# Cross attention with a second branch on one core: two staging places and the order of the last batch changed

## The chip, the cores and the metric

The kernel runs on one core of one Trainium2 chip. The metric is the device time of one execution in microseconds (us). A core has a matrix engine (PE, with weight loads shown apart as PEld), VectorE (DVE), ScalarE (ACT), GpSimd (POOL), and SyncE (SP), which here only issues transfers. SP and ACT issue DMAs; 16 DMA engines move the data.

## The reference, cut to what matters

There are 16 batches of 100 tokens x (640 wide) and a context of 722 rows (384 wide), of which the last 4 are apart. All data are float32.

```
query = x @ Wq;  key = enc @ Wk;  val = enc @ Wv          # enc: 718 context rows
hs    = attention(query, key, val)                        # 8 heads of 80
ca_q1 = (ca^T @ Wq_ca)[100 picked rows]                   # ca: the last 4 context rows
ca_hs1= attention(ca_q1, x, x)
ca_hs2= attention(ca_hs1 @ Wq, ca @ Wk_ca, ca @ Wv_ca)
out   = (hs + ca_hs2) @ Wout + b_out + x
```

## The kernel before, in words

Each float32 matrix product is done on split operands: a high part in a rounded format and a low part, the difference to the original. Nearly every tile is therefore first copied to its high part by ACT, and the low part is a subtraction on DVE or POOL. In the code `..._high` is the copy on ACT and `..._low` the subtraction. Three products (high x high, high x low, low x high) make one.

**Stage 1** (0 to some 80 us) computes the queries of all batches, transposed, in four groups of 400 columns (`query(g, j)`, j = 0 to 4 the five blocks of 128 rows, j = 5 a narrow block g, from which the second branch makes its scores). The results are split into tiles that are later used for something else: `q_out(g, j, p)` names the place. They are then stored to DRAM (`store_q2`, `store_g2`, `store_q3` on ACT's queue) and read again batch by batch. Groups 2 and 3 are not done when batch 0 starts; group 3 is woven into batch 0. The place of g of group 2 is slot 5 of `PT_keep`, columns 0 to 399, where the transposed probabilities of heads 0 to 3 come to lie in batch 0. So `pt_high(0, 0)` waits for all eight stores of group 2.

**A batch** on PE is an order written out by hand, `batch(i, first, last)`, one such function for each engine. Batch 0 is `first`, 1 to 14 are a loop, 15 is `last`. The parts are:

- `keys(i, f)`: block f of the keys, from encT (transposed context), into psS. `k_high`, `k_low` split it into kT, and SP's `lift` copies rows of kT to kstack, head by head, by DMA.
- `scores(i, h)`: head h's scores into psS, from kstack. DVE takes the row maximum (`rowmax`), ACT the exponential (`expo`), DVE divides by the sum (`norm`).
- `turn(i, h)`: PE transposes the probabilities into psT; `pt_high`, `pt_low` move them to PT.
- `context(i, u)`: a piece (u = 0 to 5) of probabilities times encN into psB; `u_high`, `u_low` move it to UT. Every piece uses the same bank of psB and waits for the `u_low` before it.
- `values(i, half)`: UT times Wv, plus the second branch, into psT; `hs_copy` on ACT and `hs_add` on DVE add its two halves and free psT. `turn` of heads 0 and 4 waits for that.
- `b2_...`: the second branch. `b2_pt_high(i, half)`, `b2_pt_low(i, half)` split its transposed probabilities of four heads.

Context pieces 2 to 5 and the values of batch i - 1 are done within batch i. Behind PE there is always the same rule: engines work strictly in the order of their function, so an instruction that waits holds all behind it on that engine.

In batches 0 to 14, `keys(i + 1, 0)` lies between `values(i - 1, 1)` and `turn(i, 4)`, and `context(i, 0)` behind `scores(i, 7)`. Batch 15 has no next keys; there `context(15, 0)` takes the place of those keys, and the output product `tile(0, 0)` starts in the place of the last keys. Wout is loaded (`load_wo`) into the room of encT, in two parts, 960 and 640 KB, and split by `wo_high` and `wo_low`. The context rows encN come in three pieces (`load_enc(i, c)`, 384 KB each); `enc_high(i, c)` on ACT is their split, and waits for `rawN{c}`.

The lines that the rows below show: 755 scores, 780 keys, 796 turn, 815 to 827 context, 848 to 855 values, 981 query blocks, 868 second-branch scores, 1190 expo, 1201 pt_high, 1219 split of encT, 1226 enc_high, 1257 b2_pt_high, 1612 rowmax, 1636 hs_add, 1675 b2_pt_low, 1772 low part of a query block, 377 load_enc, 391 and 394 lift, 500 load_wo.

Of the kernel before, what the change touches and what calls it, by code (L numbers as in the profile page):

```python
# [27 lines left out]
FT = H // 128  # L28
KT = 6
# [66 lines left out]
def program(nc, x, xT, encT, encN, caT, asel, Wq, WqT, Wk, Wv, WqcaBD, Wkca, Wvca, Wout, bout, out,  # L96
            q_d, g_d, v2_d, m_d, hs_d):

    with ExitStack() as ctx:
# [115 lines left out]
        SLOT3 = (0, 1, 2, 3, 5, 4)  # L215

        def q_out(g, j, p):

            rows = slice(0, 128 if j < FT else (2 - p) * HT)
            return PT_keep[p][rows, j, 0:GT] if g < 3 else PT_keep[p][rows, SLOT3[j], HALFCOLS]  # L220
# [43 lines left out]
        stage1_stores = "qst0 qst1 qst2 qst3a qst3b v2st mst0 mst1 mst2"  # L264
# [69 lines left out]
        with nc.Block() as block:  # L334
            @block.sync
            def _(sp):
# [172 lines left out]
                def batch(i, first=False, last=False):  # L509
                    if last:  # L510
                        load_enc(i, 0)
                    else:
                        load_encT(i + 1, 0, first)
# [7 lines left out]
                    if last:  # L521
                        sp.wait_ge(s["encT"], PARTS * (B - 1))
                        load_wo(0)
                    lift(i, 3)
                    if last:
                        load_enc(i, 2)
                    else:
# [5 lines left out]
                    if last:  # L533
                        sp.wait_ge(s["wolo"], 2)
# [9 lines left out]
                    tail_pt0(i)  # L544
                    tail_enc(i)
# [19 lines left out]
                for n, k in (("qst1", 6), ("qst2", 8), ("qst3a", 8), ("qst3b", 4)):  # L565
                    sp.wait_ge(s[n], 16 * k)
# [171 lines left out]
            def _(pe):  # L738
# [321 lines left out]
                def batch(i, first=False, last=False):  # L1060
# [40 lines left out]
                    if last:  # L1101
                        context(i, 0)
                    else:
                        keys(i + 1, 0)
# [3 lines left out]
                    if not last:  # L1108
                        context(i, 0, first)
# [73 lines left out]
            def _(act):  # L1183
# [10 lines left out]
                def pt_high(i, h, first=False):  # L1194
                    act.wait_ge(s["pt"], HEADS * i + h + 1)
                    if first and h == 0:
                        act.wait_ge(s["qst2"], 16 * 8)
                    if first and h == 4:
                        act.wait_ge(s["qst3a"], 16 * 8)
                        act.wait_ge(s["qst3b"], 16 * 4)  # L1200
# [137 lines left out]
                def wv_high(c):  # L1338
                    if c == 0:
                        act.wait_ge(s["wvin"], 16)  # L1340
                        act.wait_ge(s["q"], NP * GROUPS)
                    nc.scalar.activation(Wv_s[0][:, c, :], wv_raw[:, c, :], ACT.Copy).then_inc(s["wvhi"], 1)
# [7 lines left out]
                def store_g2():  # L1350
                    act.wait_ge(s["qlo"], NP * 2 + NP)
                    for p in range(2):
                        rows = slice(2 * p * HT, (2 + p) * HT)
                        act.dma_start(raw(g_d[rows, 2 * GT:3 * GT]), raw(q_out(2, FT, p))).then_inc(s["qst2"], 16)

                def store_q3(j):
                    to = s["qst3a" if j < 4 else "qst3b"]
# [6 lines left out]
                def batch(i, first=False, last=False):  # L1364
# [37 lines left out]
                    expo(i, 4)  # L1402
                    b2_pt_high(i, 1)
# [38 lines left out]
                    if last:  # L1442
                        wo_high(3)
# [590 lines left out]
```

## Time and profile before

| | |
|---|---|
| median of 3 runs | 975.27 us (973.79 to 976.19) |
| the profiled execution | 974.73 us |
| its span, first to last instruction | 973.0 us |
| mean granted clock of TensorE | 0.996 |
| PE busy | 960.6 us (99%), 6634 matmuls |
| DVE, ACT, POOL busy | 701.8 (72%), 491.6 (51%), 343.0 us (35%) |
| DMA queue of SP | 181.53 MB, 75.9% of 16 engines' span |
| DMA queue of ACT | 13.35 MB, 4.4% |

A table of this kind gives averages over stages with different limits. Times of single instructions are counted from the start of the span. Batch 0 runs from some 80 to 138 us, then each batch takes 50.9 us, and batch 15 lies between some 853 and 904 us. What follows is the rest of the output product.

### The profile page before, as it was taken

How to read it: one execution, taken by the hardware profiler on the slowest of the kernel's cores; microseconds unless marked ns; L12 is line 12 of the kernel's file. 1: busy time of each engine (PE TensorE's matmuls, PEld its weight loads, DVE VectorE, ACT ScalarE, POOL GpSimd, SP SyncE). 2: the span in 40 equal slices, each digit the busy share in tenths (PEclk: the TensorE clock that was granted, in tenths of full speed). 3: DMA queues.
4: the chain of work that ended last, by engine and by line, in shares of the span. 5: the costliest groups of instructions: out<-in, count | busy, mean ns of one | idle time of the engine just before them, and what ended most of it. 6: DMA issues, size and time to landing. Idle time of an engine off the chain costs nothing.

```text
span 973.0 us, 21012 instructions
## 1 busy us (share of the span) xinstructions
PE 960.6 (99%) x6634; PEld 943.3 (97%) x6634; DVE 701.8 (72%) x1260; ACT 491.6 (51%) x911; POOL 343.0 (35%) x302
## 2 busy tenths in 40 slices
PE   9999899999999999999999999999999999999998
PEld 8999899999999999999999999999999999998998
DVE  5545677777777777787777787777777777876445
ACT  6534556454555555564646363736464545555111
POOL 5223363334343425160615152433333343415000
PEclk9999999999999999999999999999999999999999
DMA  8989987797779777768796879788887978797455
GB/s 266 301 276 264 285 193 213 163 225 176 201 182 206 185 198 185 198 186 193 194 193 194 190 195 185 209 174 218 175 221 163 217 174 206 178 207 183 116 170 167
DMA packets 157625, 195.21 MB, mean 201 GB/s; under 512 B 81056, under 2 KB 111712, under 8 KB 157600
## 3 DMA queue, kind: packets, MB, share of 16 engines
q1 hardware_dynamic: 150000, 181.53, 75.9%
q10 hardware_dynamic: 7600, 13.35, 4.4%
q8 instruction: 15, 0.25, 0.1%
q14 instruction: 10, 0.08, 0.0%
HBM read 82.74 MB, written 19.95 MB: 106 GB/s over the span
## 4 chain that ended last, share of the span: by engine, by line
PE 91%; DMA 3%; SPq 2%; DVE 1%; ACT 1%; POOL 1%; issue 0%; ACTq 0%; POOLq 0%
PE psS L780 24%; PE psB L815 18%; PE psB L820 9%; PE psS L755 8%; PE psT L796 6%; PE psS L930 5%; PE psT L848 4%; PE psT L854 3%; PE psB L825 2%; PE psB L827 2%; PE psB L981 2%; DMA kstack<-kT 1%; PE psS L1055 1%; PE psB L903 1%; PE psB L880 1%; PE psT L855 1%
## 5 line engine op out<-in xcount | busy, mean ns | idle before, releaser
L780 PE MATMUL psS<-encT_keep,Wk_keep 128*128 128x360 f32 x1440 | 254.1, 329 | 0.0
L780 PEld LDWEIGHTS psS<-encT_keep,Wk_keep 128*128 128x128 f32 x1440 | 237.5, 188 | 0.7
L1190 ACT ACTIVATE probs<-psS,negmax 100x718 f32<-100x718 f32 x128 | 110.1, 860 | 131.8 <-DVE negmax L1612 131.7
L815 PE MATMUL psB<-PT_h,encN_h 128*128 128x400 f32 x480 | 169.5, 353 | 0.0
L815 PE MATMUL psB<-PT_l,encN_h 128*128 128x400 f32 x480 | 165.6, 345 | 0.0
L635 POOL TENSOR_TENSOR encT_keep<-encT_raw,encT_keep 128x718 fp32r<-128x718 f32 x45 | 83.6, 1857 | 180.7 <-ACT encT_keep L1219 176.2
L1629 DVE TENSOR_TENSOR PT_l<-psT,PT_h 128x600 fp32r<-128x600 f32 x128 | 99.6, 778 | 40.5 <-ACT PT_h L1201 36.8
L626 POOL TENSOR_TENSOR Mbd<-Mbd,fmask 128x320 fp32r<-128x320 f32 x48 | 41.8, 871 | 213.3 <-DMA Mbd<-m_split 210.7
L1612 DVE TENSOR_REDUCE negmax<-psS 100x1 f32<-100x720 f32 x128 | 114.8, 897 | 1.3 <-PE psS L755 1.3
L1201 ACT ACTIVATE PT_h<-psT 128x600 fp32r<-128x600 f32 x128 | 85.7, 669 | 42.7 <-PE psT L796 38.9
L1623 DVE TENSOR_SCALAR probs<-probs,inv 100x718 f32<-100x718 f32 x128 | 102.1, 798 | 4.5
L820 PE MATMUL psB<-PT_h,encN_l 128*128 128x400 f32 x480 | 103.6, 345 | 0.8 <-POOL encN_l L650 0.8
L1214 ACT ACTIVATE kT<-psS 128x718 fp32r<-128x718 f32 x80 | 61.6, 770 | 80.6 <-PE psS L780 78.0
L1645 DVE TENSOR_TENSOR UT<-psB,UT 128x400 fp32r<-128x400 f32 x96 | 55.1, 574 | 65.4 <-ACT UT L1243 65.3
L1243 ACT ACTIVATE UT<-psB 128x400 fp32r<-128x400 f32 x96 | 48.2, 502 | 93.8 <-PE psB L827 93.8
L1640 DVE TENSOR_TENSOR kT<-psS,kT 128x718 fp32r<-128x718 f32 x80 | 72.1, 901 | 27.1 <-ACT kT L1214 25.5
L815 PEld LDWEIGHTS psB<-PT_h,encN_h 128*128 128x128 f32 x480 | 90.3, 188 | 0.6 <-ACT encN_h L1226 0.3
L755 PE MATMUL psS<-kstack,qstack_h 120*100 120x360 f32 x256 | 87.8, 343 | 2.9 <-DMA kstack<-kT 2.9
L815 PEld LDWEIGHTS psB<-PT_l,encN_h 128*128 128x128 f32 x480 | 90.4, 188 | 0.0
L820 PEld LDWEIGHTS psB<-PT_h,encN_l 128*128 128x128 f32 x480 | 88.2, 188 | 1.2 <-POOL encN_l L650 1.2
L796 PE MATMUL psT<-ident,probs 100*128 100x100 f32 x768 | 86.9, 249 | 0.4 <-DVE P L1689 0.4
L796 PEld LDWEIGHTS psT<-ident,probs 100*128 100x128 f32 x768 | 79.3, 140 | 5.1 <-DVE P L1689 0.8
(259 smaller groups left out, 1787.4 us busy)
## 6 DMA issues: line engine op xcount, KB each, us to landing
kstack<-kT SPq DMA_DIRECT2D x64, 448.8 KB
kstack<-kT SPq DMA_DIRECT2D x192, 112.2 KB
enc_raw<-in_encN_dram SPq DMA_DIRECT2D x48, 384.0 KB, 4.6
encT_raw<-in_encT_dram SPq DMA_DIRECT2D x45, 359.0 KB, 3.9
kstack<-kT SPq DMA_DIRECT2D x32, 359.0 KB
kstack<-kT SPq DMA_DIRECT2D x32, 269.2 KB
kstack<-kT SPq DMA_DIRECT2D x32, 179.5 KB, 3.5
kstack<-kT SPq DMA_DIRECT2D x64, 89.8 KB, 3.8
```

The source lines that it names most:

```text
L635: nc.gpsimd.tensor_tensor(eT[1][:, c, :], rawT[:, c, :], eT[0][:, c, :], ALU.subtract).then_inc(s["encT"], 1)
L755: mm = pe.matmul(psS[score_slot[h]][0:S, half, 0:HALF], qst[p][:, h, :], kst[:, p, h % SLOTS, k0:k0 + HALF], start=(p == 0), stop=(p == 1))
L780: mm = pe.matmul(keys_in(f, first)[:, half, 0:HALF], w[:, c, f * 128:(f + 1) * 128], e[:, c, k0:k0 + HALF], start=(j == 0), stop=(j == 3 * ...
L796: mm = pe.transpose(psT[0:KP, k // 3, (k % 3) * S:(k % 3 + 1) * S], P[h % PRING][0:S, k * KP:(k + 1) * KP], ident[0:S, 0:S])
L815: pe.matmul(psB[:, 1, 0:RH], eN[0][:, k, cc], PT[p][:, k, rows], start=(k == 0 and p == 0), stop=False)
L820: pe.matmul(psB[:, 1, 0:RH], eN[1][:, k, cc], PT[0][:, k, rows], start=False, stop=False)
L1190: nc.scalar.activation(halves(P[h % PRING][0:S, 0:KEYS]), without_overlap(psS[score_slot[h]], S), ACT.Exp, bias=negmax[:, h:h + 1], accum_ ...
L1201: nc.scalar.activation(PT[0][:, :, h * S:(h + 1) * S].rearrange("p (a k) n -> p a k n", a=2), psT[0:KP, :, 0:3 * S].rearrange("p a (k n) - ...
L1612: nc.vector.tensor_reduce(negmax[:, h:h + 1], tile_in(h), AX.XY, ALU.max, negate=True).then_inc(s["negmax"], 1)
L1623: nc.vector.tensor_scalar(P[h % PRING][0:S, 0:KEYS], P[h % PRING][0:S, 0:KEYS], inv[:, h:h + 1], None, ALU.mult).then_inc(s["norm"], 1)
L1629: nc.vector.tensor_tensor(o[1], psT[0:KP, :, 0:3 * S].rearrange("p a (k n) -> p a k n", k=3), o[0], ALU.subtract).then_inc(s["ptlo"], 1)
L1640: nc.vector.tensor_tensor(halves(kT[f % 2][1][:, :]), without_overlap(keys_in(f, first), 128), halves(kT[f % 2][0][:, :]), ALU.subtract).t ...
```

## The change

Four things are changed.

1. g of group 2 is staged in slot 5, columns 400 to 799 of `PT_keep`, and g of group 3 in the room of the first rows of Wv (`Wv_s[p][:, 0]`), which hold the first block of Wq until the queries are done. Block 4 of group 3 goes to slot 4. The semaphores are named anew: `qst2` (q of group 2, 6 stores), `gst2` (g of group 2), `qst3` (q of group 3, 10 stores), `gst3`. `pt_high(0, 0)` waits for `qst2` alone, `pt_high(0, 4)` for `qst3` and `gst2`, `wv_high(0)` for `gst3`.
2. In batch 0, `b2_pt_high(0, 1)` stands ahead of `expo(0, 4)` on ACT and `b2_pt_low(0, 1)` ahead of `rowmax(0, 4)` on DVE.
3. In batch 15 SP issues Wout's first part at the batch's beginning, the third piece of encN behind `lift(15, 4)`, and `tail_enc` ahead of `tail_pt0`.
4. In batch 15 `context(15, 0)` stands behind `scores(15, 7)` on PE, and ACT and DVE follow: ACT does head 4's copy and exponential 7, then Wout's blocks 3 and 4, then `u_high(15, 0)`.

```diff
-        SLOT3 = (0, 1, 2, 3, 5, 4)
+        SLOT3 = (0, 1, 2, 3, 4)
         def q_out(g, j, p):
             rows = slice(0, 128 if j < FT else (2 - p) * HT)
+            if j == FT and g == 2:
+                return PT_keep[p][rows, KT - 1, HALFCOLS]
+            if j == FT and g == 3:
+                return Wv_s[p][rows, 0, 0:GT]
             return PT_keep[p][rows, j, 0:GT] if g < 3 else PT_keep[p][rows, SLOT3[j], HALFCOLS]
@@ SP, batch
                     if last:
+                        sp.wait_ge(s["encT"], PARTS * (B - 1))
+                        load_wo(0)
                         load_enc(i, 0)
...
-                    if last:
-                        sp.wait_ge(s["encT"], PARTS * (B - 1))
-                        load_wo(0)
                     lift(i, 3)
-                    if last:
-                        load_enc(i, 2)
-                    else:
+                    if not last:
                         load_encT(i + 1, 2, first)
...
                     lift(i, 4)
                     if last:
+                        load_enc(i, 2)
                         sp.wait_ge(s["wolo"], 2)
                         load_wo(1)
...
-                    tail_pt0(i)
-                    tail_enc(i)
+                    if last:
+                        tail_enc(i)
+                        tail_pt0(i)
+                    else:
+                        tail_pt0(i)
+                        tail_enc(i)
@@ PE, batch
-                    if last:
-                        context(i, 0)
-                    else:
+                    if not last:
                         keys(i + 1, 0)
                     turn(i, 4, first)
                     b2_scores2(i)
                     scores(i, 7)
-                    if not last:
-                        context(i, 0, first)
+                    context(i, 0, first)
@@ ACT
                     if first and h == 0:
-                        act.wait_ge(s["qst2"], 16 * 8)
+                        act.wait_ge(s["qst2"], 16 * 6)
                     if first and h == 4:
-                        act.wait_ge(s["qst3a"], 16 * 8)
-                        act.wait_ge(s["qst3b"], 16 * 4)
+                        act.wait_ge(s["qst3"], 16 * 10)
+                        act.wait_ge(s["gst2"], 16 * 2)
...
                         act.wait_ge(s["q"], NP * GROUPS)
+                        act.wait_ge(s["gst3"], 16 * 2)
                     nc.scalar.activation(Wv_s[0][:, c, :], wv_raw[:, c, :], ACT.Copy).then_inc(s["wvhi"], 1)
...
-                    expo(i, 4)
-                    b2_pt_high(i, 1)
+                    if first:
+                        b2_pt_high(i, 1)
+                        expo(i, 4)
+                    else:
+                        expo(i, 4)
+                        b2_pt_high(i, 1)
...
+                    if not last:
+                        enc_high(i, 2)
+                        k_high(i + 1, 0)
+                    if first:
+                        expo(i, 7)
+                    pt_high(i, 4, first)
+                    if not first:
+                        expo(i, 7)
                     if last:
                         wo_high(3)
                         wo_high(4)
-                        u_high(i, 0)
-                    else:
-                        enc_high(i, 2)
-                        k_high(i + 1, 0)
-                    if first:
-                        expo(i, 7)
-                    pt_high(i, 4, first)
-                    if not first:
-                        expo(i, 7)
-                    if not last:
-                        u_high(i, 0)
+                    u_high(i, 0)
                     pt_high(i, 5)
@@ DVE, batch
-                    rowmax(i, 4)
-                    b2_pt_low(i, 1)
+                    if first:
+                        b2_pt_low(i, 1)
+                        rowmax(i, 4)
+                    else:
+                        rowmax(i, 4)
+                        b2_pt_low(i, 1)
...
-                    if last:
-                        u_low(i, 0)
-                    else:
+                    if not last:
                         k_low(i + 1, 0)
...
-                    if not (first or last):
+                    if not first:
                         u_low(i, 0)
```

## Rows read from the trace of the kernel before

**Rows 1.** Waits of PE: engine, line, waited for, us in total, times, longest.

```profile
PE psB L981 <- DVE PT_l L1772: 2.9, 2, 2.0
...
PE psS L755 <- DMA kstack<-kT: 2.9, 2, 1.7
```

**Rows 2.** Stretches: length, busy PE PEld DVE ACT POOL, granted clock, DMA share, GB/s.

```profile
99.00:112.00 13.00, 10.07 (x65) 9.47 (x64) 8.73 (x19) 8.15 (x15) 5.21 (x3) 1.00 0.97 255
...
188.00:850.00 662.00, 662.00 (x4668) 652.47 (x4667) 511.49 (x937) 354.92 (x663) 251.73 (x208) 1.00 0.81 193
...
850.00:879.00 29.00, 29.00 (x202) 28.66 (x200) 21.87 (x40) 15.48 (x29) 5.98 (x5) 1.00 1.02 203
```

**Rows 3.** Timeline of batch 0, ACT, PE and DVE: start, length, engine, [idle before it].

```profile
85.62 1.33 ACTq L1347 DMA_DIRECT2D q_split<-PT_l  x1
...
94.41 0.50 ACT L1257 ACTIVATE P1T<-psB 100x400 fp32r<-100x400 f32 x1
...
96.92 0.67 ACT L1201 ACTIVATE PT_h<-psT 128x600 fp32r<-128x600 f32 x1 [2.02 <-DMA g_split<-PT_l]
...
101.26 0.45 PE L981 MATMUL psB<-encN_h,Wv_h 128*128 128x400 f32 x1 [1.96 <-DVE PT_l L1772]
...
106.35 0.80 ACT L1219 ACTIVATE encT_keep<-encT_raw 128x718 fp32r<-128x718 f32 x1
...
107.19 0.90 DVE L1612 TENSOR_REDUCE negmax<-psS 100x1 f32<-100x720 f32 x1
...
110.70 0.42 PE L981 MATMUL psB<-encN_h,Wv_h 128*128 128x400 f32 x1 [0.97 <-DVE PT_l L1772]
```

**Rows 4.** Chain that ended last: start, length, what; for a DMA from issue to landing.

```profile
88.78 8.06 DMA g_split<-PT_l
...
872.49 8.54 DMA kstack<-kT
```

**Rows 5.** DMA issues from 84.5 to 87 us: count, KB, us to landing.

```profile
q_split<-PT_l ACTq DMA_DIRECT2D x1, 200.0 KB, 6.1
```

**Rows 6.** Timeline of batch 15, PE.

```profile
881.17 0.38 PE L755 MATMUL psS<-kstack,qstack_h 120*100 120x360 f32 x1 [1.69 <-DMA kstack<-kT]
...
885.69 0.36 PE L815 MATMUL psB<-PT_h,encN_h 128*128 128x400 f32 x1
...
888.82 0.68 PE L796 MATMUL psT<-ident,probs 100*128 100x100 f32 x6
...
892.36 0.45 PE L815 MATMUL psB<-PT_h,encN_h 128*128 128x400 f32 x1
```

**Rows 7.** Timeline of batch 15, DMA issues on SP's queue.

```profile
862.57 0.46 SPq L500 DMA_DIRECT2D encT_raw<-in_Wout_dram  x1
...
869.41 0.52 SPq L377 DMA_DIRECT2D enc_raw<-in_encN_dram  x1
...
874.09 1.53 SPq L394 DMA_DIRECT2D kstack<-kT  x2
...
877.97 0.37 SPq L500 DMA_DIRECT2D encT_raw<-in_Wout_dram  x1
```

**Rows 8.** DMA issues in 869:870, 877:879 (batch 15) and 825:828 (batch 14), us to landing last.

```profile
enc_raw<-in_encN_dram SPq DMA_DIRECT2D x1, 384.0 KB, 9.7
...
encT_raw<-in_Wout_dram SPq DMA_DIRECT2D x1, 640.0 KB, 9.2
...
enc_raw<-in_encN_dram SPq DMA_DIRECT2D x2, 384.0 KB, 4.3
```

**Rows 9.** Timeline of batch 15, ACT and DVE.

```profile
879.59 1.57 ACT L1226 ACTIVATE encN_h<-enc_raw 128x768 fp32r<-128x768 f32 x2
...
883.02 0.86 ACT L1190 ACTIVATE probs<-psS,negmax 100x718 f32<-100x718 f32 x1 [0.41 <-DVE negmax L1612]
...
886.42 0.57 DVE L1636 TENSOR_TENSOR hs<-psT,hs 80x400 f32<-80x400 f32 x1 [2.87 <-ACT hs L1248]
```

**Rows 10.** Stretch of batch 15 behind the hole, columns as in rows 2.

```profile
882.00:886.00 4.00, 4.00 (x31) 4.00 (x30) 1.47 (x2) 1.67 (x6) 3.84 (x3) 0.57 0.68 183
```

More of the change, by code:

```diff
@@ L262, in program @@
             enc0hi enc0lo wvhi wvlo hhi hlo qhi qlo k2 k2hi k2lo v2 v2hi v2lo m mhi mlo"""
-        stage1_stores = "qst0 qst1 qst2 qst3a qst3b v2st mst0 mst1 mst2"
+        stage1_stores = "qst0 qst1 qst2 gst2 qst3 gst3 v2st mst0 mst1 mst2"
         names = " ".join((loads, products_done, exps_and_highs, steps_and_lows, splits, tails, stage1_loads, stage1,
@@ L564, in _ @@
                 batch(0, first=True)
-                for n, k in (("qst1", 6), ("qst2", 8), ("qst3a", 8), ("qst3b", 4)):
+                for n, k in (("qst1", 6), ("qst2", 6), ("gst2", 2), ("qst3", 10), ("gst3", 2)):
                     sp.wait_ge(s[n], 16 * k)
@@ L1353, in store_g2 @@
                         rows = slice(2 * p * HT, (2 + p) * HT)
-                        act.dma_start(raw(g_d[rows, 2 * GT:3 * GT]), raw(q_out(2, FT, p))).then_inc(s["qst2"], 16)
+                        act.dma_start(raw(g_d[rows, 2 * GT:3 * GT]), raw(q_out(2, FT, p))).then_inc(s["gst2"], 16)
                 def store_q3(j):
-                    to = s["qst3a" if j < 4 else "qst3b"]
+                    to = s["qst3" if j < FT else "gst3"]
                     act.wait_ge(s["qlo"], NP * 3 + j + 1)
@@ L1441, in batch @@
                         enc_high(i, 1)
-                    if last:
-                        wo_high(3)
-                        wo_high(4)
-                        u_high(i, 0)
-                    else:
+                    if not last:
                         enc_high(i, 2)
@@ L1453, in batch @@
                         expo(i, 7)
-                    if not last:
-                        u_high(i, 0)
+                    if last:
+                        wo_high(3)
+                        wo_high(4)
+                    u_high(i, 0)
                     pt_high(i, 5)
@@ L1846, in batch @@
                         rowmax(i, 7)
-                    if last:
-                        u_low(i, 0)
-                    else:
+                    if not last:
                         k_low(i + 1, 0)
```

## The prediction

> **What bounds the kernel now.** I read the waits of the matrix engine first, then busy time by stages, then the two places with waits in order of time, and last the landings of transfers. The waits [rows 1] are few. The stages [rows 2] show why: from 188 to 850 us PE is busy in all 662 us, although its transfers keep the DMA engines at 0.81 and DVE is at 77%. So only what moves the few holes of PE moves the end. The holes that the diff can reach lie in batch 0 (13 us from 99 us on with 10.07 us busy) and in batch 15 (from 879 us on). From 850 to 879 us PE is full but the DMA share is 1.02: the queue has no spare time there. All sums are made on the profiled execution, 974.73 us (span 973.0 and 1.7 around it); the median of the runs is 975.27, 0.5 above it.
>
> **Batch 0, g of group 2 in another place.** ACT ends the copy of head-half 0 of the second branch at 94.41 + 0.50 and then stands 2.02 us until 96.92 for the store of g of group 2 [rows 3], which landed at 88.78 + 8.06 = 96.84 [rows 4]. Behind that copy hang, in order, the subtraction, row maximum 3, exponential 3 and the split of query block (3,1); block (3,2) starts at 101.26 with 1.96 us of hole. After the change the copy waits for the stores of q alone. The last of these is issued at 85.62 [rows 3] and lands 6.1 us later, at 91.7 [rows 5], 3.2 us before ACT is ready. So the whole chain comes 2.0 us earlier and the hole goes: -1.96 us. The wait for g of group 2 moves to head 4's copy at 124 us, 27 us behind its landing: 0. The stores of group 3 keep sources, sizes and order but for g, whose buffer is first rewritten by the split of Wv some 12 us after its store is issued: 0 (at the other end, one store latency of 8 us, if it were late). No instruction is added; lines that only rename semaphores cost 0.
>
> **Batch 0, head-half 1 of the second branch ahead of exponential 4.** Now row maximum 4 starts at 107.19. Its new forerunner on DVE needs an ACT copy that sits behind the split of encT: 106.35 + 0.80, less the overlap of about 0.1, gives 107.05; + 0.50 for the copy + 0.57 for the subtraction = 108.1 [rows 3]. Row maximum 4 is thus 0.9 later, exponential 4 starts at 109.0 and ends at 109.85, the split of query block (3,3) is 0.50 on ACT and 0.57 on DVE, and block (3,4) starts at about 110.95, not at 110.70 [rows 3]. So this hole grows by 0.25; with the third piece of encT perhaps a tenth late, since everything now comes 2 us sooner, I take +0.35 (bounds: -0.1, if DVE finds the copy ready, and +0.9, the whole delay). Batch 0: -1.96 + 0.35 = -1.6 us. Nothing later in batch 0 gives it back: the stall for the low part of encN hangs on ACT's work after block (3,5) and comes along. In batches 1 to 14 the code is the same.
>
> **Batch 15, the transfers.** Head 6's scores wait 1.69 us, until 881.17 [rows 6], for the lift of key block 4, which landed at 872.49 + 8.54 = 881.03 [rows 4]. Two things are taken from in front of it: Wout's first 960 KB are issued at about 855, ahead of encN's first piece, instead of 862.6, and the third piece of encN (384 KB, now issued at 869.41) goes behind the lifts, to about 875.7, where the last of them (issue from 874.09, 1.53 us) is out [rows 7]. The first gains next to nothing: the queue is full from 850 us on [rows 2], so the same bytes still stand ahead of the lift; it only makes encN's first two pieces land later, and ACT wants those at 878 us. The second is worth what the piece takes. It landed at 869.41 + 9.7 = 879.1 [rows 8], and the 404 KB of head 6's lift 1.93 us after it: 209 KB per us. So 384 KB are 1.8 us, head 6's lift lands near 879.2, and the hole of 1.69 closes (I take 0.1 left; bounds 0 and 1.7).
>
> But now the third piece is late. Ahead of it stand also head 7's lifts, 449 + 112 + 112 KB = 673 KB: at the same rate 3.2 us. Same bytes, other order: it lands where head 7's lift lands today, 881.03 + 3.2 = 884.2. A second reading agrees: Wout's second part (640 KB, issued 877.97) lands 9.2 us later at 887.2 [rows 8]; the 6.1 us from 881.03 hold 673 + 640 KB, 215 per us, head 7's share 3.1 us. Bounds: 880.3 with the 4.3 us that such pieces take in a batch with a quiet queue [rows 8], and 885.4 with today's 9.7. I take 884.2, since the queue is full to the last issue.
>
> ACT reaches that piece's split at about 880.35, halfway through the pair that starts at 879.59 and ends near 881.1 [rows 9], and its place is not changed. Behind it in ACT's order stand the copy of XM, exponential 5, XM's high part, exponential 6 and the copy of values' output; DVE's row maximum 6 stands behind the XM sum. Exponential 6 starts at 883.02 [rows 9], 1.95 us after the pair; about 0.2 of that is the wait for the late scores, so the work between is 1.75.
>
> **Batch 15, the context's first piece.** Its 3.13 us (885.69 to 888.82) [rows 6] lie today between values and the transposes of head 4. Both use psT, and in that time ACT and DVE empty it: the copy, then the subtraction from 886.42 for 0.57, end 886.99 [rows 9], 1.3 us after values. Moved behind head 7's scores, the piece leaves the 1.3 us bare, and more: the copy stands in ACT's order behind exponential 6. With the piece at 884.2: split 0.75, the 1.75 to exponential 6, its 0.86, and 1.1 for copy and subtraction: 4.5 us. Head 4's transposes start at 888.7. Values ended near 882.6, so PE stands 6 us.
>
> From there: transposes, second-branch scores and head 7's scores 2.0 us (888.82 to about 890.8 now), the context piece 3.13: 893.8. Piece 1 needs piece 0's psB emptied, and only head 5's transposes (0.45) and the turned parts (0.36) lie between, so its 1.3 us show: 895.1, against 892.36 now [rows 6]: +2.7 us. ACT's two splits of Wout are moved to just before that copy; they end at about 894.0, just in time. The short wait for c2's copy ahead of 892.36 is gone, and in the 2.7.
>
> **The clock.** [...] Bounds: 0 (the 1.96 us hole before 101.26 was followed by full clock, 1.00 over 99 to 112 [rows 2]) and twice 1.7. [...] The trace shows one hole with a fall and one without; I leave (b) its 0.13.
>
> Batch 15: +2.7 + 1.7 = +4.4. Sum: 974.73 - 1.6 + 4.4 = 977.5 in a profiled execution, 978.0 as a median. Conversion of all figures below: + 0.5.
>
> **The rivals.**
> (a) The queue empties sooner and the third piece is on time. For it: pieces in quiet batches land in 4.3 us, and Wout is out of the way by 863. Against: DMA share 1.02 up to 879. Then values end at 882.6 and head 4's transposes start near 884.8 (exponential 6 at 882.8, then 0.86 + 1.1), piece 1 near 891.2, -1.2 us. Total -1.6 - 1.2 = -2.8: 972.5; with a fall of clock 974.2.
> (b) It is late, but the clock stays up: -1.6 + 2.7 = +1.1: 976.4.
> (c) The first hole doesn't close, because the stores of q land later than 91.7 or the wait only changes its name. The landing speaks against it. Then +1.6 on the forecast: 979.6.
> The point from which (a) and the forecast part: with the clock's fall, the two edits balance when the third piece lands at 884.2 - 2.8 = 881.4 us on today's axis.
>
> [...]
>
> **How the numbers follow.** Forecast (late piece, clock falls once) 0.60, (a) 0.20, (b) 0.13, (c) 0.07. The time is 978.0. The forecast's own range is 976 to 980 (piece 883 to 885, clock 1 to 2.5). The range 972.8 to 980.2 takes in (a) and (c) and leaves the extremes. A measurement can tell about 0.3%, 2.9 us, from no change. Above 978.2 lie nearly half of the forecast and (c): 0.34. Below 972.4 lies a third of (a) and little else: 0.12. Between them: 0.54.
>
> **What would show it.** Right: ACT's split at line 1226, third piece, with 3 to 4 us of idle before it and a transfer as releaser; PE idle 5 to 6 us before head 4's transposes (line 796) in batch 15, then a clock near 0.5; no wait for g_split near 95 us; block (3,2) about 2 us earlier, block (3,4) 1.6 earlier. Wrong: the third piece landing within 5 us of its issue, no hole longer than 2.5 us in batch 15, or a new hole in batches 1 to 14.

## The result

The changed kernel takes 980.42 us (median of 20 runs, 973.84 to 986.25) against 974.40 us for the kernel before in the same session (20 runs, 971.31 to 981.19). The ratio of the two is 1.0048, interval 1.0028 to 1.0068: slower by about half a per cent, 4.7 us (2.7 to 6.6). The profiled execution took 976.48 us, with a span of 974.8; the one before took 974.73 with 973.0.

The forecast was 978.0, +2.7 us, and 977.5 in a profiled execution. The direction and the place came out as said. The profiled time is 1.0 under its forecast, the median 2.4 over it. On the 975.27 us of before that the forecast started from, the ratio gives 980.0, just inside the upper end of the range (980.2); the median as measured, 980.42, lies just outside it. And 0.48% is past the 0.3% that part no change from slower: the case that had 0.34, not the 0.54.

First the waits of PE in the changed kernel (line, what was waited for, us in total, times, longest). In this kernel's file the lines stand 3 to 6 further down: the transposes are L802, the context L821 to L833, the query blocks L987.

```profile
PE psT L802 <- DVE hs L1642: 4.9, 1, 4.9
...
PE psB L987 <- DVE PT_l L1778: 1.4, 1, 1.4
...
PE psS L761 <- DMA kstack<-kT: 0.3, 1, 0.3
```

In [rows 1] the two waits for PT_l summed to 2.9 us; one of 1.4 is left. The waits for the stacked keys, 2.9 with a longest of 1.7, are down to 0.3. In their place stands one of 4.9 us, before head 4's transposes. The changed kernel's stretches (length, busy PE, PEld, DVE, ACT, POOL, granted clock, DMA share, GB/s) say where:

```profile
99.00:112.00 13.00, 11.57 (x78) 10.98 (x77) 7.60 (x14) 6.03 (x13) 4.73 (x3) 1.00 1.00 295
...
879.00:892.00 13.00, 8.06 (x49) 7.85 (x48) 6.27 (x13) 6.18 (x13) 5.21 (x4) 0.74 0.57 173
888.00:890.00 2.00, 2.00 (x8) 1.95 (x7) 1.22 (x4) 0.00 (x0) 0.00 (x0) 0.50 0.32 99
```

Batch 0 is fuller (11.57 busy of 13 against 10.07 in [rows 2]). In batch 15 PE is busy 8.06 us of 13, at a mean clock of 0.74. The last row is full of matmuls, at a granted clock of 0.50.

To see where the time between the spans went, I compare the same instruction in the two traces. The kernel before, key blocks on PE and a stretch of stage 1 (columns as above):

```profile
30.00:40.00 10.00, 10.00 (x63) 9.97 (x64) 4.20 (x4) 4.04 (x7) 0.00 (x0) 0.83 1.06 354
...
95.65 3.14 PE L780 MATMUL psS<-encT_keep,Wk_keep 128*128 128x360 f32 x18
...
130.77 3.21 PE L780 MATMUL psS<-encT_keep,Wk_keep 128*128 128x360 f32 x18
...
855.42 3.14 PE L780 MATMUL psS<-encT_keep,Wk_keep 128*128 128x360 f32 x18
```

The same of the changed kernel, with block (3,4) of the query:

```profile
30.00:40.00 10.00, 10.00 (x71) 10.00 (x72) 4.20 (x4) 4.03 (x8) 0.00 (x0) 1.00 1.06 357
...
93.74 3.14 PE L786 MATMUL psS<-encT_keep,Wk_keep 128*128 128x360 f32 x18
...
107.11 0.42 PE L987 MATMUL psB<-encN_h,Wv_h 128*128 128x400 f32 x1 [1.43 <-DVE PT_l L1778]
...
127.63 0.29 PE L921 MATMUL psB<-ident,P2x 100*96 100x100 f32 x1 [0.28 <-DVE P2x L1717]
127.69 3.22 PE L786 MATMUL psS<-encT_keep,Wk_keep 128*128 128x360 f32 x18
...
852.71 3.14 PE L786 MATMUL psS<-encT_keep,Wk_keep 128*128 128x360 f32 x18
```

Changed minus before: -1.91 us at 95.65; -3.59 at block (3,4) (110.70 in [rows 3]); -3.08 at 130.77; -2.71 at 855.42; and +1.76 at the context's piece 1 (892.36 in [rows 6], 894.12 now), as at the end (+1.8). So the changed stretch of batch 0 gave -1.68, the rest of batch 0 took back 0.5, batches 1 to 14 took back 0.4 more, and batch 15 cost 4.5. The first -1.91 is not the change's: that code is untouched but for names. Most of it is a stretch of stage 1 that ran at a mean clock of 0.83 in the one execution and 1.00 in the other (10 x 0.17 = 1.7). Without it the changed stretches cost +3.7 us in this pair of traces (-1.68 + 0.5 + 0.4 + 4.5).

Batch 15 of the changed kernel in detail (start, length, engine, [idle before it and its releaser]), and the transfer as the chain of waits has it (start of the issue, us to landing):

```profile
880.84 0.84 ACT L1229 ACTIVATE encN_h<-enc_raw 128x768 fp32r<-128x768 f32 x1 [3.08 <-DMA enc_raw<-in_encN_dram]
...
883.26 0.86 ACT L1193 ACTIVATE probs<-psS,negmax 100x718 f32<-100x718 f32 x1 [0.16 <-DVE negmax L1618]
...
884.63 0.57 DVE L1642 TENSOR_TENSOR hs<-psT,hs 80x400 f32<-80x400 f32 x1 [0.72 <-ACT hs L1251]
...
885.34 1.23 PE L802 MATMUL psT<-ident,probs 100*128 100x100 f32 x6 [4.94 <-DVE hs L1642]
...
888.91 0.54 PE L821 MATMUL psB<-PT_h,encN_h 128*128 128x400 f32 x1
...
894.12 0.45 PE L821 MATMUL psB<-PT_h,encN_h 128*128 128x400 f32 x1 [0.33 <-DVE UT L1651]
```

```profile
854.70 12.59 DMA kstack<-kT
...
874.69 6.13 DMA enc_raw<-in_encN_dram
```

Read it from the top. The third piece of encN was issued at 874.69 and landed 6.13 us later, at 880.82. ACT had waited 3.08 us for it. Exponential 6 follows from 883.26, then the copy of values' output, and the subtraction on DVE, which frees psT at 885.2. PE has stood 4.94 us by then. The six transposes then take 1.23 us where they took 0.68 in [rows 6], and the context's first matmul 0.54 where it took 0.36 there.

### The profile page after: what moved, and what is told of

It reads as the page before. It is cut to its first block, busy times and chain, and to the rows that moved or that the text cites. A ratio compares the mean times of both kernels' runs of the same rounds, so it can differ in the third digit from the quotient of the medians.

```text
span 974.8 us, 21013 instructions
## 1 busy us (share of the span) xinstructions
PE 961.2 (99%) x6634; PEld 942.9 (97%) x6634; DVE 706.1 (72%) x1260; ACT 492.2 (50%) x911; POOL 344.1 (35%) x302
## 4 chain that ended last, share of the span: by engine, by line
PE 90%; SPq 3%; DMA 2%; DVE 2%; ACT 1%; issue 1%; POOL 1%; ACTq 0%; POOLq 0%
PE psS L786 22%; PE psB L821 17%; PE psB L826 9%; PE psS L761 8%; PE psT L802 6%; PE psS L936 5%; PE psT L854 4%; PE psT L860 2%; PE psB L987 2%; DMA kstack<-kT 2%; PE psB L831 2%; PE psB L833 2%; SPq L398 1%; PE psB L909 1%; PE psS L1061 1%; PE psB L886 1%
## 5 line engine op out<-in xcount | busy, mean ns | idle before, releaser
L821 PE MATMUL psB<-PT_h,encN_h 128*128 128x400 f32 x480 | 169.9, 354 | 0.3 <-DVE UT L1651 0.3
L821 PE MATMUL psB<-PT_l,encN_h 128*128 128x400 f32 x480 | 166.0, 346 | 0.0
L802 PE MATMUL psT<-ident,probs 100*128 100x100 f32 x768 | 87.5, 250 | 4.9 <-DVE hs L1642 4.9
L821 PEld LDWEIGHTS psB<-PT_h,encN_h 128*128 128x128 f32 x480 | 90.7, 189 | 1.1 <-DVE UT L1651 0.4
L821 PEld LDWEIGHTS psB<-PT_l,encN_h 128*128 128x128 f32 x480 | 90.8, 189 | 0.0
L802 PEld LDWEIGHTS psT<-ident,probs 100*128 100x128 f32 x768 | 79.5, 141 | 9.8 <-issue 5.3
```

Of the source, the lines that this page charges most:

```text
L802: mm = pe.transpose(psT[0:KP, k // 3, (k % 3) * S:(k % 3 + 1) * S], P[h % PRING][0:S, k * KP:(k + 1) * KP], ident[0:S, 0:S])
L821: pe.matmul(psB[:, 1, 0:RH], eN[0][:, k, cc], PT[p][:, k, rows], start=(k == 0 and p == 0), stop=False)
```

## The experiments

Eleven kernels ran, one of them twice (e2 and e11), each time in 12 runs beside 34 or 35 of the kernel before; e9 to e12 ran on another chip than e1 to e8. All holes (stretches in which PE stands) are from their profiled executions, one for each.

### e1: batch 0 as changed, batch 15 as before

```
  batch(15) on SP, PE, ACT and DVE: order of the kernel before
```

> Batch 0 as changed (g of groups 2 and 3 in other places, head-half 1 ahead of exponential 4 and row maximum 4), batch 15 wholly as before. Theory: the hole before query block (3,2) (1.96 us before) is gone, the one before block (3,4) grows to 1.3 to 1.4 us, the end comes 1.6 us sooner (ratio 0.998). Rival (the loss of the changed kernel lies in batch 0, through stores that land later): slower than before by 2 us or more, ratio above 1.002, and a wait for q_split or g_split ahead of head 0's or head 4's copy.

976.90 us, ratio 1.0011 (0.9989 to 1.0032), 973.69 profiled: neither the 0.998 of the theory nor the rival's 1.002 is settled. The hole before block (3,2) is gone, but before block (3,4) stands a larger one (batch 0, PE and ACT; then a stretch behind it):

```profile
100.37 1.82 ACTq L1367 DMA_DIRECT2D q_split<-PT_l  x1
...
102.24 0.67 ACT L1205 ACTIVATE PT_h<-psT 128x600 fp32r<-128x600 f32 x1 [1.75 <-issue]
...
103.94 0.81 ACT L1223 ACTIVATE encT_keep<-encT_raw 128x718 fp32r<-128x718 f32 x1 [1.02 <-DMA encT_raw<-in_encT_dram]
...
105.65 0.90 DVE L1621 TENSOR_REDUCE negmax<-psS 100x1 f32<-100x720 f32 x1
...
108.69 0.42 PE L985 MATMUL psB<-encN_h,Wv_h 128*128 128x400 f32 x1 [3.28 <-DVE PT_l L1781]
```

```profile
110.00:112.00 2.00, 2.00 (x7) 1.99 (x7) 0.33 (x1) 0.34 (x2) 0.00 (x0) 0.50 1.07 354
```

ACT's split of encT's third piece waits for its transfer. Head-half 1's copy stands behind the split, and with the new order row maximum 4 stands behind that copy, so the transfer is now on the way to block (3,4). In the kernel before, row maximum 4 did not hang on ACT's split. The transfer accounts for 1.02 us here. Some 0.7 us more come from ACT itself: issuing one store took it 1.82 us, where the same issue takes 1.11 us in the changed kernel, so the copy at 102.24 starts 0.99 us behind block (3,3) and not 0.27. The changed kernel has the same batch 0 and a hole of 1.43. The 3.28 us hole was followed by a granted clock of 0.50 (110 to 112 us).

### e2 and e11: g's places alone, twice

```
  g_split of groups 2, 3: new places and semaphores
  (exponential 4, row maximum 4 and batch 15: order of the kernel before)
```

> As e1, but exponential 4 and row maximum 4 stay ahead of head-half 1 as before: only the places of g are changed. Theory: the first hole is gone, the second stays 0.9 to 1.0 us, so the end comes 2.0 us sooner than before and 0.4 sooner than e1 (by the holes; the times can hardly tell e1 from e2). Rival (the reorder is what shortens the chain): the hole before block (3,4) is larger than 1.4 us.

> g of groups 2 and 3 in the new places, nothing else; the kernel of an earlier run again, on this chip, beside the one with the split of encT moved. Theory A (the gain of 0.24% is the hole of up to 2 us before query block (3,2)): ratio 0.996 to 0.999 again, below 1 with its interval, and no hole before block (3,2). Theory B (the earlier ratio was chance, since the hole is not in every run of the old places): ratio 0.999 to 1.001.

First 971.60 us, ratio 0.9976 (0.9955 to 0.9998); the second time 974.21, ratio 1.0001 (0.9979 to 1.0023). Together that is about 0.999: a gain of 0.1%, and no run settles whether it is there. Neither trace has a hole before block (3,2), but the one before block (3,4) is 1.48 and 1.18 us, not the 0.9 to 1.0 that e2 was to have. Why so little is gained shows in the traces of kernels with g in its old place. In e3 and e4 there is no hole there at all, and in e12 ACT waits 0.47 us and PE 0.40:

```profile
94.28 0.67 ACT L1200 ACTIVATE PT_h<-psT 128x600 fp32r<-128x600 f32 x1 [0.47 <-DMA g_split<-PT_l]
...
98.61 0.45 PE L980 MATMUL psB<-encN_h,Wv_h 128*128 128x400 f32 x1 [0.40 <-DVE PT_l L1771]
```

So the same code had holes of 1.96, 0.40, 0 and 0 us in four profiled executions (before, e12, e3, e4). The profile of before showed the largest of them. What differs is the landing of g's store: 8.06, 6.5, 4.1 and 5.8 us behind its issue.

### e3: SP's order of batch 15 alone

```
+ wait encT; load_wo(0)          before load_enc(15, 0)
+ load_enc(15, 2)                behind lift(15, 4), not before it
+ tail_enc(15); tail_pt0(15)     in this order
```

> Only SP's order of batch 15 is changed (Wout's first part at the beginning, third piece of encN behind the lifts); context piece 0 stays between values and head 4's transposes. Theory: the hole before head 6's scores falls from 1.7 to under 0.5 us; ACT waits 3 us for the third piece; PE is busy 3.1 us with the context's piece meanwhile if its splits allow, but piece 0 needs the split of that same third piece, so PE stands 2 to 3 us before context piece 0. End +0 to +2 us, ratio 1.000 to 1.002. Rival (the lateness of the third piece costs nothing, the moved context is all of the loss): faster than before by 1.7 us or more.

975.04 us, ratio 1.0006 (0.9982 to 1.0031), 972.99 profiled. The hole before head 6's scores is gone; the third piece is late by 0.82 us, not by 3, and PE doesn't stand before the context's first piece. But a later wait shows (ACT; then DVE, and PE before head 5's transposes):

```profile
880.39 0.85 ACT L1228 ACTIVATE encN_h<-enc_raw 128x768 fp32r<-128x768 f32 x1 [0.82 <-DMA enc_raw<-in_encN_dram]
...
882.69 1.95 DVE L1686 TENSOR_TENSOR XM<-P,XM 100x256 fp32r<-100x256 f32 x1
...
886.16 1.95 DVE L1625 TENSOR_SCALAR probs<-probs,inv 100x718 f32<-100x718 f32 x1
...
889.60 0.56 PE L798 MATMUL psT<-ident,probs 100*128 100x100 f32 x4 [2.22 <-DVE P L1691]
```

Here the 0.82 us cost PE nothing: the context's first piece still stood behind values, and psT was emptied under it. The 2.22 us are mostly not the transfer's. DVE works without a break from 882.69 to head 5's transposes, and three of its operations take 4.8 us (1.95, 0.89, 1.95) where they take 1.5 in the kernel before (0.65, 0.25, 0.60). Such long ones come in every trace (last section).

### e4: only the context's first piece moved

```
- context(15, 0) before turn(15, 4)
+ context(15, 0) behind scores(15, 7)
  wo_high(3), wo_high(4), u_high(15, 0) and u_low(15, 0) behind it, as in the change
```

> Only the context's piece 0 is moved behind head 7's scores (with ACT's and DVE's order); SP's order as before, third piece on time. Theory: the hole of 1.7 us before head 6's scores stays; PE stands some 1.5 to 2.5 us before head 4's transposes (psT to be emptied behind exponential 6), 0.3 to 0.6 us before piece 1. End +1 to +2 us against before, ratio 1.001 to 1.002. Rival (the transfers are all of the loss): no hole over 0.5 us before head 4's transposes, ratio 1.000.

976.34 us, ratio 1.0029 (1.0008 to 1.0049), 973.68 profiled. With the third piece on time the move alone bares both waits that the forecast named, the emptying of psT and of psB (PE, batch 15):

```profile
883.99 0.28 PE L796 MATMUL psT<-ident,probs 100*128 100x100 f32 x1 [1.28 <-DVE hs L1631]
...
884.29 1.97 DVE L1618 TENSOR_SCALAR probs<-probs,inv 100x718 f32<-100x718 f32 x1
...
891.32 0.45 PE L815 MATMUL psB<-PT_h,encN_h 128*128 128x400 f32 x1 [1.24 <-DVE UT L1640]
```

1.28 + 1.24 = 2.5 us, which is 0.26% of the time; the ratio says 0.29%. That they agree is in part chance. The 1.28 comes again in e5. The second wait is 0.52 in e5 and 0.51 in e6, which have the same code there: in this trace a normalization on DVE took 1.97 us and not 0.60, and exponential 7, Wout's splits and the copy of piece 0 came later by it. Still this is the only single part of the change whose interval lies above 1.

### e12: only Wout's first part at the beginning of batch 15

```
+ wait encT; load_wo(0)          before load_enc(15, 0)
```

> Only Wout's first part moved to the beginning of batch 15; all else as before. Theory A (forecast: the queue is full, the same bytes stand ahead of the lifts, so nothing is gained or lost): ratio 1.000, the hole before head 6's scores about 1.1 to 1.8 us. Theory B (Wout ahead holds up the lift of head 4 and the early pieces of encN, as the changed kernel's trace suggests with 12.6 us from issue to landing): key block 4's split waits 1.3 us for the lift and encN's first pieces land 12 to 13 us after issue; if PE feels it, a new hole of about 1 us before head 5's or 6's scores, ratio 1.001 to 1.002.

974.51 us, ratio 1.0000 (0.9974 to 1.0026). Both theories get something. ACT's split of key block 4 waits for a lift, as in the changed kernel (1.28 there), and PE does not feel it:

```profile
868.02 0.77 ACT L1213 ACTIVATE kT<-psS 128x718 fp32r<-128x718 f32 x1 [1.47 <-DMA kstack<-kT]
...
878.67 0.38 PE L754 MATMUL psS<-kstack,qstack_h 120*100 120x360 f32 x1 [1.23 <-DMA kstack<-kT]
```

In the traces with Wout in its old place that split waits for PE only, 0.34 to 0.36 us. Of the six with Wout ahead five have it wait for a lift (0.92 to 1.65 us; e3 has 0.35). The early load costs no time that a run shows, but it isn't harmless: in the changed kernel a lift just behind it takes 12.59 us.

### e5: the changed kernel with the third piece ahead of the lifts

```
+ load_enc(15, 2)                before load_encT / lift(15, 4)
- load_enc(15, 2)                behind lift(15, 4)
```

> The changed kernel with one thing undone: the third piece of encN is issued ahead of lift(15, 4) again; Wout's first part stays at the beginning, the context's piece 0 behind head 7's scores. Theory (the long hole is the late third piece): ACT's split of it no longer waits, the hole of 4.9 us before head 4's transposes falls to 1.3 to 2.2 us, the one before head 6's scores is back (0.5 to 1.7 us), the end 2 to 3 us sooner than the changed kernel, ratio to before 1.002. Rival (the hole is the bare emptying of psT alone): it stays over 4 us.

977.47 us, ratio 1.0032 (1.0007 to 1.0056), 979.48 profiled (PE, batch 15):

```profile
884.49 0.38 PE L762 MATMUL psS<-kstack,qstack_h 120*100 120x360 f32 x1 [2.31 <-DMA kstack<-kT]
...
890.48 0.70 PE L803 MATMUL psT<-ident,probs 100*128 100x100 f32 x6 [1.28 <-DVE hs L1643]
```

The hole before head 4's transposes falls from 4.94 to 1.28, which is what e4 has: so by this comparison 3.66 us of it are the late piece and 1.28 the bared emptying of psT. The hole before head 6's scores comes back, with a granted clock of 0.50 behind it (886 to 888 us). In both orders the transfer that is put second costs a hole, 2.31 us here and 3.66 in the changed kernel; the median gains some 0.16%, within the intervals.

### e6: the changed kernel with the hole filled

```
+ 30 matmuls of 400 columns, result not used, between values(14, 1) and turn(15, 4)
```

> The changed kernel with 30 matmuls of 400 columns added on PE in batch 15 between values and head 4's transposes, into a bank that the context's piece 0 overwrites. At full clock they take 5.5 us, about as long as the hole of 4.9. Theory (the hole costs twice, once as such and once by the clock that falls behind it): the granted clock stays at 1.00 from there to piece 1, so the work from the transposes to the end of piece 0 takes 5.1 us instead of 7.6, and the end comes 1.5 to 2 us sooner than the changed kernel although work was added. Rival (the clock's fall is hidden by other waits): the end comes later than the changed kernel's by the 0.6 us that the filling is too long.

979.09 us, ratio 1.0057 (1.0035 to 1.0079), 976.70 profiled (PE and DVE of batch 15, and a stretch):

```profile
882.25 5.59 PE L1111 MATMUL psB<-Wv_h 128*128 128x400 f32 x30
...
885.60 0.57 DVE L1645 TENSOR_TENSOR hs<-psT,hs 80x400 f32<-80x400 f32 x1 [0.68 <-ACT hs L1254]
...
887.68 0.68 PE L802 MATMUL psT<-ident,probs 100*128 100x100 f32 x6
...
894.25 0.45 PE L821 MATMUL psB<-PT_h,encN_h 128*128 128x400 f32 x1 [0.51 <-DVE UT L1654]
```

```profile
884.00:890.00 6.00, 6.00 (x43) 5.96 (x42) 3.30 (x8) 2.08 (x5) 2.27 (x2) 1.00 0.77 226
```

With PE busy the clock stayed at 1.00 from 884 to 890 us, where the changed kernel had 0.50. From head 4's transposes to piece 1 it takes 894.25 - 887.68 = 6.57 us, against 894.12 - 885.34 = 8.78 in the changed kernel: the lower clock cost 2.2 us there. Yet the kernel is not measurably faster. As an estimate I take (1 - granted clock) x span of a run as the time that it lost to the lower clock. Over the timed runs that is 2.4 us on average instead of 5.1, and the rest of the time rose by nearly as much (977.4 against 975.0 us). The trace shows how: psT was free at 886.17, when the subtraction on DVE ended (885.60 + 0.57), but the filler held PE until 887.68. So the filling was 1.5 us too long here and spent most of the 2.2 that the clock gave back. A shorter filling wasn't tried.

### e9: the changed kernel without its reorder of batch 0

```
  batch 0: expo(0, 4); b2_pt_high(0, 1)   and   rowmax(0, 4); b2_pt_low(0, 1)   as before
```

> The changed kernel with exponential 4 and row maximum 4 of batch 0 ahead of the second branch's head-half 1 again. Theory A (the reorder of batch 0 costs about 0.3%, since the third piece of encT lands in front of row maximum 4, and my forecast had it at 0.35 us): the time falls to about 977.0, ratio near 1.0013 to 1.002 of the kernel before, and the profile has row maximum 4 ahead of the wait for encT's third piece. Theory B (the reorder is worth 0.35 us as predicted, and batch 15 has the whole loss): about 979.5 to 980, ratio near 1.004. In both the third piece of encN in batch 15 keeps ACT waiting 2 to 3 us and PE stands 4 to 5 us before head 4's transposes.

977.73 us, ratio 1.0035 (1.0010 to 1.0061), 976.96 profiled. The median lies between the theories and the intervals cover both: the difference of the ratios, 0.13%, is well within them. Batch 15 repeats the changed kernel's trace to a few tenths (ACT, PE, and a stretch of 2 us):

```profile
881.20 0.84 ACT L1229 ACTIVATE encN_h<-enc_raw 128x768 fp32r<-128x768 f32 x1 [3.21 <-DMA enc_raw<-in_encN_dram]
...
885.71 1.23 PE L802 MATMUL psT<-ident,probs 100*128 100x100 f32 x6 [5.07 <-DVE hs L1638]
```

```profile
884.00:886.00 2.00, 0.29 (x2) 0.32 (x3) 1.21 (x5) 0.96 (x3) 1.59 (x1) 0.59 0.28 56
```

So batch 15, with g's places that gain about 0.1%, makes 1.0035 without the reorder: it holds most of the loss.

### e7 and e10: the split of encT's third piece moved back

```
  batch 0, ACT:  encT_high(1, 2) behind q_high(3, 3), no longer before exponential 4
  e7 on top of e1, e10 on top of g's places alone
```

> As e1 (batch 0 as changed, batch 15 as before), but the split of encT's third piece for batch 1 is moved behind the split of query block (3, 3), so head-half 1, row maximum 4 and exponential 4 no longer stand behind that transfer. Theory (the reorder of e1 loses by putting row maximum 4 behind the landing of encT's third piece): the hole before block (3,4), 3.3 us in e1 and 1.5 in e2, is 0.3 to 1.0 us, and the time is that of e2 or 0.5 us better, ratio 0.997 to before. Rival (it is the second-branch copy itself): hole 1.4 us or more.

> g of groups 2 and 3 in the new places and, in batch 0, the split of encT's third piece moved behind the split of query block (3,3); all else as before. Theory A (that split's wait for its transfer, 1.0 to 2.3 us in the runs seen, lies on the way to exponential 4 and block (3,4)): the hole of 1.48 us before block (3,4) closes to under 0.5, and the time is about 1 us under the kernel with g's places alone (970.6 against 971.6), ratio near 0.9965. Theory B (ACT's next work there waits for DVE and PE anyway, or row maximum 4 sets the time): equal to g's places alone, ratio 0.9975, hole still above 1 us.

e7: 972.79 us, ratio 0.9989 (0.9965 to 1.0014). e10: 971.74 us, ratio 0.9981 (0.9958 to 1.0004), the lowest of the series but for e2's first time. Before block (3,4) (e7, then e10, batch 0 on PE):

```profile
106.65 0.42 PE L985 MATMUL psB<-encN_h,Wv_h 128*128 128x400 f32 x1 [1.17 <-DVE PT_l L1782]
```

```profile
107.15 0.42 PE L985 MATMUL psB<-encN_h,Wv_h 128*128 128x400 f32 x1 [1.18 <-DVE PT_l L1778]
...
880.56 0.38 PE L759 MATMUL psS<-kstack,qstack_h 120*100 120x360 f32 x1 [2.38 <-DMA kstack<-kT]
```

e7's hole is 1.17 where e1's was 3.28. It was to be 0.3 to 1.0, and the ratio 0.997. ACT's split was the way by which the transfer reached PE; as the changed kernel has 1.43 with the split in its place, e7 can't be credited with the whole 2.1. In e10 nothing went: the hole was 1.18 in e11 too. There my theory A was wrong, since row maximum 4 did not hang on that split without the reorder. In e11 the split didn't wait for its transfer at all. Where it did wait without the reorder (1.19 us in e9, 2.00 in e8, 2.29 in e2) the hole was 1.32, 1.52 and 1.48, so a late transfer cost 0.3 us at most there. About 1.2 us are left whatever the order.

### e8: the third piece between the lifts of heads 6 and 7

```
  on top of g's places alone, in batch 15:
  lift(15, 4, heads=(6,)); load_enc(15, 2); lift(15, 4, heads=(7,))
```

> e2 (only the places of g changed) with the third piece of encN in batch 15 issued between the lifts of head 6 and head 7; everything else of batch 15 as before. Theory (the queue works in order of issue, about 209 KB per us): head 6's lift lands 1.8 us earlier and the hole of 1.8 us before its scores closes to under 0.3; the third piece lands where head 6's lift did, 1 us or less after ACT is ready for it, and context piece 0 hides that. End 1.5 us sooner than e2, ratio 0.996 to before. Rival (landings don't follow the order of issue): the hole stays over 1 us.

973.38 us, ratio 1.0001 (0.9977 to 1.0025), 971.65 profiled. No hole before head 6's scores, as its theory had it; but one further on (PE, batch 15), and the ratio isn't the 0.996 that was expected:

```profile
885.25 0.45 PE L832 MATMUL psB<-PT_h,encN_h 117*128 117x400 f32 x1 [1.08 <-DMA encN_l<-enc_raw]
```

1.76 us in e2 against 1.08 here. The new wait isn't this order's alone: e11 and e12 have it too, with 0.71 and 1.10 us. As a version it doesn't beat the kernel before.

## Why the forecast was right, step by step

**The third piece of encN: right.** It was to land at 884.2 on the axis of before; it landed at 880.82, which is 883.5 when the 2.7 us by which the changed kernel is ahead there are added. ACT's idle was to be 3 to 4 us and was 3.08, with the transfer as releaser. PE's hole was to be 5 to 6 and was 4.94; e5 splits it into 3.66 for the piece and 1.28 for the moved context. Rival (a), the piece on time, is out; its nearest neighbour is e3, where the piece was 0.82 late. By that spread (0.82 to 3.21 us in four traces) the size was a draw, too. The piece put behind the lifts was late in every trace that has it (3.08, 0.82, 2.03 and 3.21 us of ACT's idle in the changed kernel, e3, e6 and e9). That it would land behind them was an estimate from the landings in the kernel before, which came in the order of issue: the third piece at 879.1, the lift behind it at 881.03, Wout at 887.2 [rows 4, 8].

**The context's piece: right in the sum.** Piece 1 was to come at 895.1 + 1.7 = 896.8 on the axis of before, and came at 894.12 + 2.7 = 896.8. The parts differ: the transposes came 0.7 earlier than forecast, the clock took 2.2 instead of 1.7, and the way from the transposes to piece 1 is 6.57 us at a clock of 1.00 (e6) where the forecast had 6.4. The emptying of psB took its 1.3 us (from 892.76, when piece 0 ended, to 894.06, when the subtraction 893.49 + 0.57 did), and head 5's transposes and the turned parts covered all but 0.33 of it.

**The clock: right in kind.** Rival (b) is out: 0.50 from 888 to 890 behind a hole of 4.94 us, and e9 repeats it behind 5.07 us (0.50 from 886 to 890); shorter holes differ (last section). No run shows the sum's 1.7 us for the changed kernel; it was an estimate from the kernel before, whose 4 us at 0.57 [rows 10] come to 4 x 0.43 = 1.7. In its place the profile showed 2.2 us (8.78 from the transposes to piece 1, 6.57 at a clock of 1.00 in e6). In the timed runs it is more. The time lost to the lower clock, reckoned as for e6, is on average 5.1 us for the changed kernel (20 runs), 3.5 for e9, and 1.5 to 2.1 for the kernel before (three sets of 34 or 35). The changed kernel's profiled execution, with 0.996, had 3.9. So 3.0 to 3.6 us more than before go to the lower clock in the timed runs, by this reckoning.

**Head 6's scores: right.** The hole of 1.69 closed. The wait of ACT for key block 4's lift (1.28 us) was not foreseen. That Wout's earlier place "gains next to nothing" holds for the lift that I looked at, not for the one just behind Wout; its cost on PE was zero (e12).

**Batch 0, block (3,4): right, with a stranger in it.** The stretch was to gain 1.6 us and gained 1.68, with the hole at 1.43 (0.97 + 0.46; forecast +0.35, bound 0.9). The traces part the 0.46. It holds a short operation of DVE ahead of row maximum 4 that took longer (before, then changed):

```profile
105.52 0.24 DVE L1619 TENSOR_SCALAR probs<-probs,inv 100x39 f32<-100x39 f32 x1
```

```profile
101.48 0.64 DVE L1625 TENSOR_SCALAR probs<-probs,inv 100x39 f32<-100x39 f32 x1
```

With the old order and 0.24 us for it the hole is 0.97 and 1.02 (before, e12); with the old order and 0.62 to 0.64 it is 1.18 to 1.20 (e3, e4, e10, e11); with the reorder and 0.64 it is 1.43 to 1.45 (changed kernel, e5, e6). So the reorder costs 0.25 us, as the sum had it, and the other 0.2 is that operation, which the sum did not have. The term was worked out for a third piece of encT that is nearly in time. In e1 it was 1.02 late, and the hole 3.28. "Nothing later in batch 0 gives it back" was wrong by 0.5 us: part of it is the new wait of 0.28 before line 921. The rest is not traced.

**The -1.96 us of the first hole: mis-sized.** This is the term that was most wrong. The hole was real in the profile of before, and closed as forecast, so rival (c) is out. But it is not a property of the kernel: the same code showed 0.40, 0 and 0 in other executions, and g's places alone gain about 0.1% over two measurements, near 1 us. A forecast of a median may take only the mean of such a hole. With -0.6 (the mean of the four, 2.36 / 4) in place of -1.96 it would have been 979.4, 0.6 below the 980.0 that the ratio gives.

**What was luck.** The profiled time came within 1.0 us of its forecast, but 1.9 us of its lead were gained in stage 1, which the change doesn't touch. The changed stretches cost 3.7 us in the trace where the sum had 2.8: batch 15 came out as forecast (4.5 for 4.4), and the 0.9 is what the rest of batch 0 and batches 1 to 14 took back.

**What stays open.** Why the median lies 3.9 us over the profiled execution of the same kernel. The clock accounts for 1.2 of it (5.1 against 3.9). No trace shows the other 2 to 3 us. The holes vary between executions by such amounts (1.17, 1.18 and 3.28 before block (3,4); 0.65, 1.76 and 2.38 before head 6's scores in e11, e2 and e10, which are alike in batch 15). They can also come where the traces of before and of the changed kernel have none, in batches 1 to 14: there PE stood 3.5 us in e11 and not at all in e2, the same kernel, and 0.6 to 1.3 in e5, e7 and e10. With the fall in stage 1 that makes most of the 6.3 us between the profiled executions of e11 and e2 (976.99 and 970.74). So a profile in which these batches are full is no proof that they always are. That the changed kernel has more of its work behind such transfers would explain it, but isn't shown. What took back the 0.4 us in batches 1 to 14 isn't traced either.

The parts add up roughly: e4 +0.29%, e3 +0.06% (Wout in it 0.00), e1 +0.11%, which is g's -0.1 and the reorder's +0.2 (the traces show 0.03% for it while encT's piece is in time); together +0.46% against a measured +0.48%. Each has an interval of 0.2% on either side, so this is a check and no proof. Of all runs only e2's first lies below 1 with its interval, by 0.02%, and e11 didn't repeat it; e10 is the next.

## To carry to other kernels

In the full queue of batch 15 (DMA share 1.02 in [rows 2]) the lifts, put ahead of the third piece, closed a hole of 1.69 us, and the piece behind them opened one of 3.66: price the wait of the last in the row, and what stands on its engine behind it, before counting the gain of the first. Work that stands between two users of one buffer is cover for the emptying; before moving it, read how long the emptying takes (here 1.3 us for psT and again for psB). And a hole that ends on a transfer's landing may be a draw, as the one before block (3,2) was (1.96, 0.40, 0 and 0 us in four executions): before crediting its removal in full, look at it in a second execution of the same code.

## What the runs showed of the hardware that was not expected

**Holes and the clock.** A hole of one size was followed by a lower clock in one trace and not in another. These are all the holes of 1.6 us and more in the fourteen traces, with the granted clock behind them. It fell to 0.50 behind 1.69 (before), 1.84 (e3, before head 0's scores), 2.21 (e5, the same place), 2.31 (e5), 2.38 (e10), 3.28 (e1), 4.94 (changed kernel) and 5.07 us (e9). It stayed at 1.00 behind 1.75 (e4), 1.76 (e2), 1.96 (before) and 2.22 us (e3). The rows of e2 and e10, two kernels that have the same code there:

```profile
878.00:884.00 6.00, 5.73 (x47) 5.58 (x47) 4.14 (x7) 3.34 (x9) 5.70 (x4) 1.00 0.65 183
```

```profile
882.00:884.00 2.00, 2.00 (x16) 2.00 (x15) 2.00 (x2) 0.95 (x2) 1.86 (x2) 0.50 0.67 183
```

A fall also came in stage 1 without such a hole: 0.83 over 30 to 40 us, with PE busy in that stretch, in the kernel before, e5, e6 and e11, and none in the other ten, in code that none of these kernels changes. All that the four show before it is 0.29 to 0.49 us of idle before the matmuls at 23.35 to 23.50 us; e3 has 0.39 there and no fall.

**Transfers.** The third piece of encN took 7.2 to 11.1 us to land in the nine traces that issue it ahead of the lifts (9.7 in [rows 8]), 7.1 between them (e8) and 5.1 to 6.8 in the four behind them. In the changed kernel a lift just behind Wout took 12.59 us, where other lifts of that batch took 8.3 to 9.0.

**VectorE beside GpSimd.** One and the same operation of DVE took between 0.60 and 2.1 us. The normalization of one head (100x718) runs 1792 times in the fourteen traces. It took 0.60 us whenever GpSimd was idle, without exception. In 360 cases it took 0.8 to 2.1 us, and in every one of them GpSimd was at work for about half of its time or more; the other 201 with that much work of GpSimd beside them took 0.60 all the same. The forecast has no such term. Long operations of this kind made 0.2 us of the hole in batch 0, 0.7 of the 1.24 in e4 and most of the 2.22 in e3, with GpSimd at work beside each. What in GpSimd's work decides it was not tried.
